# Degree factors spread by matmuls with repeated columns instead of diagonals, and ScalarE's first table load placed ahead of its first copy

## The reference, cut to what matters

```python
def gcn_conv(x, src, dst, W, b):
    h = x @ W
    s, d = concat(src, loop), concat(dst, loop)
    deg = segment_sum(ones, d, num_segments=n)
    dinv = rsqrt(maximum(deg, 1.0))
    msgs = h[s] * (dinv[s] * dinv[d])[:, None]
    return segment_sum(msgs, d, num_segments=n) + b

h = leaky_relu(gcn_conv(x, src, dst, W1, b1), 0.2)
x = layernorm(x + gcn_conv(h, src, dst, W2, b2) * sigmoid(ctx @ Wg + bg) + ctx @ Wb)
# two relational layers, each: relu(segment_sum(xt[rel, src], dst) + x @ SW + b)
```

## Time and profile before

| | |
|---|---|
| Median of three runs | 1705.29 us (1701.72 to 1708.20) |
| Profiled execution, its own time | 1705.26 us |
| Span of its trace, first to last instruction | 1703.1 us |
| PE, POOL, DVE, ACT busy | 87%, 55%, 45%, 32% of the span |
| Mean granted TensorE clock | 0.967 |

### The profile page before, as it was taken

How to read it: one execution, slowest core, us unless ns; L and a number is a source line. 1 busy time by engine, 2 the same in 40 slices (tenths; PEclk the granted TensorE clock), 3 DMA queues, 4 the chain that set the end, 5 groups by cost and what they waited for, 6 DMA issues and landing times.

```text
span 1703.1 us, 24985 instructions
## 1 busy us (share of the span) xinstructions
PE 1486.8 (87%) x9602; PEld 921.5 (54%) x9602; DVE 773.7 (45%) x2381; ACT 540.4 (32%) x764; POOL 939.1 (55%) x963
## 2 busy tenths in 40 slices
PE   1367989999878989999989899968999989998995
PEld 1345554444435556566656565634666656665663
DVE  8999972224656656567566765510000111011001
ACT  1365530001345555566465655510000000000000
POOL 6600000000077777777777777717777677757755
PEclk9997999999979999999999999979999999999997
DMA  4311341253545546565466555546656555555631
GB/s 131 115 79 78 156 175 77 104 212 117 205 154 177 185 162 216 174 223 212 141 216 220 185 175 203 192 173 223 221 215 219 199 178 209 211 192 197 224 122 48
DMA packets 69791, 294.31 MB, mean 173 GB/s; under 512 B 20644, under 2 KB 26510, under 8 KB 55844
## 3 DMA queue, kind: packets, MB, share of 16 engines
q1 hardware_dynamic: 39236, 230.26, 34.9%
q0 software_dynamic: 30432, 62.39, 13.4%
HBM read 165.63 MB, written 126.94 MB: 172 GB/s over the span
## 4 chain that ended last, share of the span: by engine, by line
PE 65%; POOL 10%; DVE 10%; DMA 8%; issue 6%; ACT 2%; POOLq 0%; DVEq 0%; SPq 0%; ACTq 0%
PE ps L1329 32%; PE ps L1213 9%; PE ps L1350 8%; DVE hot_mem L1606 7%; PE ps L1301 5%; POOL acc L762 5%; DMA acc<-table_rel,edges 4%; POOL node_id L762 3%; PE ps L1243 2%; DMA node_id<-table_rel,edges 2%; PE ps L1388 2%; PE ps L1374 2%; POOL acc L706 1%; ACT blocks L934 1%; POOL xT L706 1%
## 5 line engine op out<-in xcount | busy, mean ns | idle before, releaser
L762 POOL DMA_INDIRECT node_id<-table_rel,edges x453 | 439.3, 970 | 530.9 <-DMA table_rel<-node_id 372.2
L762 POOL DMA_INDIRECT acc<-table_rel,edges x453 | 441.6, 975 | 182.0 <-issue 131.7
L1329 PE MATMUL ps<-blocks,raw 128*128 128x512 f16 x1350 | 407.3, 381 | 0.0
L1329 PE MATMUL ps<-blocks,dinv 128*128 128x512 f16 x1200 | 387.0, 386 | 13.7 <-issue 13.7
L934 ACT ACTIVATE blocks<-ps 128x800 f16<-128x800 f32 x384 | 317.4, 838 | 216.6 <-PE ps L1301 215.5
L1350 PEld LDWEIGHTS ps<-raw,acc 128*128 128x128 f32 x996 | 187.6, 196 | 107.7 <-issue 50.5
L1350 PEld LDWEIGHTS ps<-raw,node_id 128*128 128x128 f32 x1026 | 193.0, 195 | 93.6 <-issue 28.4
L1329 PE MATMUL ps<-blocks,edges 128*128 128x512 f16 x600 | 231.5, 386 | 0.0
L1855 DVE TENSOR_SCALAR hot_mem<-cell_h,rel_cols 128x400 f16<-128x400 f16 x768 | 228.5, 338 | 0.0
L1852 DVE TENSOR_SCALAR hot_mem<-cell_h,rel_cols 128x128 f16<-128x128 f16 x768 | 166.4, 271 | 135.0 <-PE ps L1301 133.0
L1301 PE MATMUL ps<-hot_mem 128*128 128x400 f16 x768 | 193.0, 337 | 19.4 <-ACT blocks L934 16.5
(11 more groups left out here) (183 smaller groups left out, 1279.1 us busy)
## 6 DMA issues: line engine op xcount, KB each, us to landing
rcounts<-blocks SPq DMA_DIRECT2D x48, 1600.0 KB, 6.3
blocks<-rcounts SPq DMA_DIRECT2D x48, 1600.0 KB, 7.7
counts<-blocks SPq DMA_DIRECT2D x6, 3200.0 KB, 10.1
blocks<-counts SPq DMA_DIRECT2D x6, 3200.0 KB, 10.5
table_rel<-node_id SPq DMA_DIRECT2D x50, 256.0 KB, 2.1
table_rel<-xn SPq DMA_DIRECT2D x50, 256.0 KB, 2.4
node_id<-table_rel,edges POOLq DMA_INDIRECT x453
acc<-table_rel,edges POOLq DMA_INDIRECT x453
```

The source lines that it names most:

```text
L762: nc.gpsimd.indirect_dma_start(got[m % GATHERS][:, j, :], None, tables_rel[layer - 2], bass.IndirectOffsetOnAxis(ap=row_i[:, first + j:fir ...
L1329: last = nc.tensor.matmul(ps[:, bank, 0:2 * HCOLS], part, half_pairs[u % 2][:, :, t * HCOLS:(t + 1) * HCOLS], start=(k == 0), stop=(k == T ...
```

## The change

`make_diag` and its seven DVE instructions are gone. `spread_dinv` now builds the same rows from 128-column products: the stationary operand is one column of `dinv_col` repeated 128 times, the moving one the identity. For each of the two groups q of a block and each place a there is one product, written to every second column of the PSUM bank. A full block takes four such products in place of one of 512 columns; the last block takes two of 64. PE waits for a new semaphore `roots_ready`, set by the reciprocal at h = 23, once at g = 0; DVE's own wait behind this reciprocal is gone with it. ACT gets a one-column copy (`warm`) behind its wait for the patterns, in front of which its first table load now stands.

```diff
@@ ScalarE
             act.wait_ge(patterns_ready, 5)
+            nc.scalar.activation(warm[:, :], strip_node[:, 0:1], ACT.Copy)
@@ TensorE
             def spread_dinv(g):
                 if g == 0:
                     pe.wait_ge(mode_ready, 1)
+                    pe.wait_ge(roots_ready, 1)
                 else:
                     pe.wait_ge(dinv_copied, g)
-                pe.wait_ge(diag_ready, g + 1)
-                nc.tensor.matmul(ps[:, SPREAD_BANK, 0:block_width(g)], ones[:, :], tin[:, g * BANK:g * BANK + block_width(g)],
-                                 start=True, stop=True).then_inc(dinv_spread, 1)
+                spread_to = ps[:, SPREAD_BANK, :].rearrange("p (q c a) -> p q c a", q=2, a=PAIR)
+                for q, group in enumerate(range(2 * g, min(2 * g + 2, GROUPS))):
+                    rows = min(P, (block_width(g) - q * PAIR * P) // PAIR)
+                    for a in range(PAIR):
+                        last = nc.tensor.matmul(spread_to[:, q, 0:rows, a], dinv_col[:, group, a:a + 1].to_broadcast([P, P]), ident[:, 0:rows],
+                                                start=True, stop=True)
+                last.then_inc(dinv_spread, 1)
@@ VectorE
-            def make_diag(g):
-                n = block_width(g) // (PAIR * P) or 1
-                rows = block_width(g) // (PAIR * n)
-                nc.vector.tensor_tensor(tin[:, g * BANK:g * BANK + block_width(g)].rearrange("p (q c a) -> p q c a", q=n, a=PAIR),
-                                        ident[:, 0:rows].unsqueeze(1).unsqueeze(3).to_broadcast([P, n, rows, PAIR]),
-                                        dinv_col[:, 2 * g:2 * g + n, :].unsqueeze(2).to_broadcast([P, n, rows, PAIR]),
-                                        ALU.mult).then_inc(diag_ready, 1)
...
                 if h == ROOTS_AT + 2:
                     dve.wait_ge(degrees_sqrt, 1)
-                    then(nc.vector.reciprocal(dinv_col[:, :, :], dinv_col[:, :, :]))
+                    nc.vector.reciprocal(dinv_col[:, :, :], dinv_col[:, :, :]).then_inc(roots_ready, 1)
...
                 for g in range(XG):
-                    if h == DIAG_AT + 2 * g:
-                        make_diag(g)
                     if h == TURN_AT + 2 + 2 * g:
                         scale_x(g)
```

More of the change, by code:

```diff
@@ L311, in gnn_kernel @@
         eps = sb("eps", [P, 1])
+        warm = sb("warm", [P, 1])
         degrees = sb("degrees", [P, GROUPS, PAIR])
@@ L341, in gnn_kernel @@
         deg_ready, deg_sqrt, tin_ready = sem("deg_ready"), sem("deg_sqrt"), sem("tin_ready")
-        diag_ready, dinv_spread, dinv_copied, scaled = (sem(n) for n in ("diag_ready", "dinv_spread", "dinv_copied", "scaled"))
+        roots_ready, dinv_spread, dinv_copied, scaled = (sem(n) for n in ("roots_ready", "dinv_spread", "dinv_copied", "scaled"))
         feat_done, high_ready, rest_ready, mid_ready, low_ready = (
@@ L485, in gnn_kernel @@
         KEYS_TURNED, RELS_TURNED = {1: 5, 2: 15, 3: 20}, 28
-        GATE_AT, ROOTS_AT, DIAG_AT, TURN_AT = 20, 21, 30, 32
+        GATE_AT, ROOTS_AT, TURN_AT = 20, 21, 32
         def early_products(h):
```

## The result

In runs on one chip, side by side, the changed kernel took 1700.39 us (median of 10, 1696.49 to 1703.41) and the kernel before 1707.75 us (median of 10, 1701.72 to 1717.76). The ratio is 0.9955, 95% interval 0.9933 to 0.9976: 7.4 us less, with 4.1 to 11.4 us in the interval. The forecast was 1702.1 us, 3.2 us less than before, and within 0.5%. That 1700.39 lies so near to 1702.1 is partly luck: the kernel before measured 1707.75 in these ten runs, 2.5 us over the median of three that the forecast started from, and the difference is more than twice the forecast one. Ratios and their intervals leave out a few runs that were much longer at a lower granted clock (one of e3's took 1820.33 us at 0.84); medians are of all runs.

What follows compares the result with a forecast made beforehand. DVE was taken to set the pace where the diagonals lie, PE behind the loop. 1705.26 − 3.20 (diagonals) + 0.05 (first spread) = 1702.1 us; the forecast's own range 1698 to 1706, with rivals 1696.5 to 1708.

Steps and rivals of the forecast that it cites:

- DVE's diagonals: In the loop, where DVE sets the pace: removing the seven diagonal instructions gains 3.20 us, bounds 0 to 3.80.
- g = 2 to 6: Later blocks' diagonals on DVE: 0.60 us gained for each of four, 0.20 for the short last one.
- g = 0: First block's diagonal on DVE, at h = 30: gain 0.60 us; its slower spread on PE costs 0.05.
- DVE's dropped wait behind the reciprocal: DVE need not wait for the reciprocal's end: worth 0.08 us once, left out of the sum.
- g = 1: Second block's diagonal, ahead of `scale_x(0)`: gain 0, as the wait for ACT's copy grows from 0.41 to 1.01 us.
- The cover of the later blocks: Steady part: ACT's copy of the spread still ends 2.35 us before `scale_x` without the diagonal.
- The spread: PE's 128-column products cost 0.03 us more for a block; 0.05 counted for the first, none elsewhere.
- The table load: ACT's first table load, 1.28 us at 21.75, moves earlier: gain 0, at most 1.28.
- the marker: DVE's long run of hots begins at 154.8 instead of 158.03 us; a shift under 2 or over 5 refutes.
- rival 1: At the first dense products: the clock rises no earlier, the gain is given back, 1703.9 to 1705.3 us; chance 0.17.
- Rival 3: Denser PE work shortens the low-clock stretches, sparing DVE's 0.71 us wait: 1697 to 1700 us; chance 0.10.

Runs made afterwards that it cites:

- e3: The changed kernel with the seven diagonals kept on DVE at their old places, unread: 1706.54 us, ratio 0.9994 to the kernel before.
- e4: As e3, but each diagonal written three times, the two additional ones into an idle buffer: 1711.25 us, ratio 1.003 to the kernel before.
- e1: The changed kernel without the early copy `warm`: 1702.94 us, ratio 0.9976 to the kernel before.
- e8: The changed kernel with 216 fp16 products added ahead of the loop (contiguous output, strided output, repeated stationary column): 1987.32 us in one run.
- e2: The kernel before with only the early copy `warm` added: 1707.42 us, ratio 1.0009 to the kernel before.
- e11: The changed kernel with spread and ACT's copy one pair earlier, as e7, run again: 1981.72 us, ratio 0.9998 to the kernel before.
- e9: The changed kernel unaltered, run a third time: 1979.22 us, ratio 0.9972 to the kernel before.
- e10: The changed kernel without `warm`, run again beside e9: 1985.27 us, ratio 1.0002 to the kernel before.
- e5: The changed kernel unaltered, run a second time: 1982.2 us, ratio 1.0006 to the kernel before.
- e6: The changed kernel without `warm`, run again beside e5: 1978.91 us, ratio 0.9968 to the kernel before.
- e7: The changed kernel with PE's spread and ACT's copy of each block one pair earlier: 1979.34 us, ratio 0.9983 to the kernel before.
- e12: The changed kernel unaltered, run a fourth time: 1996.69 us, ratio 1.0013 to the kernel before.

## Why the prediction was right, and where it was not

**DVE's diagonals (predicted 3.20 us, measured 3.3; the whole change in the loop 3.5).** In the kernel that keeps them the loop is as long as before but for 0.2 us (e3), and each one that is added costs what the theory says in the steady part (e4). By its parts:

- g = 2 to 6, predicted 2.60. From `scale_x(0)` to DVE's long run of hots, less the wait ahead of that run, before needs 158.03 − 112.39 − 0.71 = 44.93 us, and e1, where such a wait stands too, 153.25 − 110.51 − 0.40 = 42.34. That is 2.59. The row of e1:

```profile
153.25 76.27 DVE L1612 TENSOR_TENSOR hot_mem<-hot_mem,edges 128x2048 f16<-128x2048 f16 x94 [0.40 <-PE ps L1077]
```

- g = 0, predicted 0.60, less 0.05 for the slower spread. From the reciprocal to `scale_x(0)` before needs 21.89 us, e3 21.69, after 21.06. The diagonal is the 0.6 between the last two. The 0.2 between the first two is DVE's dropped wait behind the reciprocal, as the rows above place it. I had put it at 0.08 and left it out, arguing that PE's fault sums would hold DVE up again. They do, by 0.15 us before and in e3 alike, but they come 0.19 earlier too. No run changes this wait alone.
- g = 1, predicted 0, with `scale_x(0)` waiting 1.01 us: it waits 0.97.
- The cover of the later blocks, predicted 2.35 us: in after a steady copy ends at 131.05 (ACT's line 836 at 130.45, 0.60 us), 2.21 before the `scale_x` at 133.26.

**The spread (predicted 0.03 us more for a block, 1.77 at the low clock).** 1.06 us busy instead of 1.02, and 1.67 at the low clock. The argument was that an fp32 column takes 1.7 ns, so that PSUM gets one column in four cycles. e8 agrees with it from the other side: where columns come every cycle the same stride doubles the time. One reading there was loose: 1061 to 596 ns and 563 to 276 ns are not "the same factor" but 1.8 and 2.0. It changed no term. The Trainium skill's page "PSUM — Partial Sum Buffer", in "Specifications (TRN2)", says that a non-contiguous access pattern slows matmuls significantly. For dense fp16 products at 2.4 GHz e8 agrees (109 to 214 ns). For the spread's fp32 products the trace does not (1.02 to 1.06 us).

**The table load (predicted 0).** Right, by e1 and e2. The 0.33 us of slack between the last copy and the first hots was enough to say so.

**The step that failed** is the one on the marker in the trace: DVE's long run of hots was to begin at 154.8 instead of 158.03 us, and a shift under 2 or over 5 us was to show the prediction wrong, whatever the median says. After has no wait in front of this run. In all kernels that have the wait, 79.50 to 79.54 us lie between the run's start and the 75 products, so its place after is 231.58 − 79.53 = 152.05: a shift of 6.0. Three things were wrong with the marker. It was counted from the start of the span, and 1.70 us of the shift come before the loop. It stood behind a wait of 0.71 that can vanish; over the seven executions without diagonals it takes values from none to 1.09, and 0.71 to 0.86 in the three with them. And 0.4 us more than the sum came from the loop itself. (1.70 + 0.71 + 3.20 + 0.4 makes the 6.0.) By its own test the prediction fails, though its mechanism in the loop holds.

**Rivals 1 and 3, the clock.** Both said that the low stretch at the start of the dense products would move or change its length. The wait there does change, but in one and the same kernel too: in the changed one from none to 1.09 us. Nothing was given back on the mean of the seven executions without diagonals (0.43 us, against 0.76 with): rival 1 falls. Rival 3 came true in the profiled execution in part, by 0.71 us of wait and 3.43 us behind the loop. That second part isn't the change's, as the same stretch shows in other kernels. From the first 75 products to that DMA it takes 225.2 us in after, e4 and e11, 225.6 in e9, 227.7 in e10, and 228.4 to 229.1 in before, e1, e2, e3, e5, e6, e7, e8 and e12. One piece of it shows in the chains above: 14 products of the tables took 8.15 us before and 6.07 after. In their windows (columns as in the earlier trace rows) the granted clock is 0.79 before,

```profile
440.00:456.00 16.00, 12.13 (x26) 5.30 (x25) 9.37 (x26) 4.99 (x10) 0.00 (x0) 0.79 0.46 173
```

and 1.00 after:

```profile
433.00:449.00 16.00, 11.91 (x32) 5.15 (x31) 10.36 (x29) 6.53 (x13) 0.00 (x0) 1.00 0.57 214
```

The changed kernel itself shows both: the 14 products take 6.07 us in e9 and 8.30 in e12. e4, which has more diagonals than any kernel, had the short value, and e1, with none, the long one. A link between fewer diagonals and a higher clock here is not there in these executions. There is one with the wait in the loop: the nine executions in which DVE waits at the first dense products all have the long value, and four of the five without that wait (after, e4, e9, e11; not e10) the short one. What decides it is open, and with four executions that have diagonals so is whether the change makes the short value more frequent.

**The 1.70 us of the start.** The timeline before has DVE waiting for gathered rows,

```profile
73.64 0.74 DVE L1531 TENSOR_SCALAR acc<-xT 128x768 int32<-128x768 int32 x1 [1.22 <-DMA xT<-in_src,gather_at]
```

and the one after has the same instruction without a wait:

```profile
72.37 0.55 DVE L1538 TENSOR_SCALAR acc<-xT 128x768 int32<-128x768 int32 x1
```

The wait is there in e2 (1.26) and e3 (1.06), not in e1 and e4. In the later sets it is 5.6 to 5.8 us in e5, e10 and e11, and none in e6, e7, e9 and e12. It goes neither with the diagonals nor with `warm`.

**What stays open** is the size of the median's change. The loop gives 3.5 us, e1 measured 4.1 (2.0 to 6.3), the changed kernel 7.4, and its interval (4.1 to 11.4) leaves both 3.2 and 3.5 just outside. e9 with 5.6 (1.6 to 9.5) and e5 and e12 near nothing don't decide. The interval of the first set (0.9933 to 0.9976) and that of e12 (0.9983 to 1.0044) don't even meet, for one and the same change, so a ratio varies between sets by more than its interval says. The profiles show two sources of several microseconds that the change doesn't touch, the gathers' wait and the low-clock stretch behind the loop. That they were kinder to the changed kernel in those ten runs is argued, not shown. So the mechanism rests on the loop; why the median moved by 7.4 us and not by 3.5 no run explains.

No version here beats the changed kernel measurably. The earlier spread takes 0.6 us off the loop in two traces, which is under what the times can tell.

## What to carry to other kernels

DVE held a tenth of the span's chain, yet each instruction taken off it was worth the 0.60 us that it held in the chain, in the stage where DVE ran without gaps, and nothing ahead of a wait that grew by as much: judge by the stage, and count them one by one. Check a forecast of a few microseconds by the distance of two events close to the edit with the waits subtracted, in several kernels: here it repeats within 0.3 us, while medians and single spans move by 7. Place such a marker behind an event near the edit, not at the start of the span, and not behind a wait.

## What the runs showed of the hardware

- PSUM output to every second fp32 column: 214 ns instead of 109 for 256 dense fp16 columns at 2.4 GHz, 1.06 instead of 1.02 us for a spread of 512 fp32 columns (e8 and the trace after).
- A stationary operand read as one column 128 times costs nothing (111 ns against 109, e8).
- The granted clock in the records reads 1.00 in 108 to 112 us of the kernel before, where the spread's products took up to 1061 ns as at the low level, and 596 later; in e8 it reads 1.00 from 13 to 34 us, for the 213 ns products and for the 109 ns ones. In these two stretches the durations say more than the record.
- One and the same kernel took 1706 us in one set of runs and 1983 to 1997 in others, at a granted clock of 0.97 and 0.91. It isn't the chip: the same one had 1706.0 in the set of e1 to e4 and 1997.03 in that of e12. The loop without its waits kept its length within 0.3 us all the same. Some 4 to 12 us went into the time before it (the reciprocal starts at 94.7 to 100.5 us instead of 88.8 to 90.6), the rest into the stages behind it, and differences of a few microseconds could no longer be measured there.
